# Quantised rows of the later chunk pairs: transposed by DMA in place of TensorE and ScalarE

## What is computed

```python
x = x + tanh(g_xattn[0]) * xattn(layernorm(x), ctx_1024, ctx_1024, Wq, bq, Wk, bk, Wv, bv, Wo, bo)
x = x + tanh(g_ffn[0]) * ffn(layernorm(x), w1, b1, w2, b2)

def _quant_per_tensor(x):
    scale = jnp.maximum(jnp.max(jnp.abs(x)), MIN_RANGE) / QP          # QP = 127
    return (_ste_round(x / scale), scale)
def _qlinear(x2d, w, b):
    xq, sx = _quant_per_tensor(x2d)
    wq, sw = _quant_per_tensor(w)
    out = jnp.matmul(xq, wq.T) + b[None, :]
    return out * (sw * sx)
h = gelu(_qlinear(x, w1, b1))          # 4096 x 2048
o = _qlinear(h, w2, b2)                # 4096 x 512
```

## Time and profile before

| | |
|---|---|
| three runs, us | 675.15, 672.69, 674.81; median 674.81 |
| profiled execution, us | 677.12, its span 675.2 |
| mean granted clock of TensorE | 0.955 |
| busy share of the span | PE 86%, DVE 74%, ACT 47%, POOL 27% |
| busy in step 0, 421.0 to 453.0 us | PE 31.01, DVE 23.11, ACT 24.84; DMA share 0.61 |
| in step 1, 453.0 to 482.9 | PE 29.84, DVE 27.67, ACT 23.07; DMA share 0.75 |
| in step 2, 482.9 to 513.7 | PE 30.70, DVE 29.72, ACT 23.07; DMA share 0.72 |
| in step 3, 513.7 to 541.5 | PE 27.80, DVE 21.91, ACT 19.26, POOL 11.12; DMA share 0.76 |

### The profile page before, as it was taken

One profiled execution on the slowest core, in us unless ns is written; L12 is line 12 of the kernel. 1 busy time (PEld: TensorE's weight loads), 2 busy tenths in 40 slices (PEclk: granted clock), 3 DMA queues, 4 the chain that ended last, 5 costly groups with the idle time before them and its releaser, 6 DMA issues. The chain is left out here.

```text
span 675.2 us, 9643 instructions
## 1 busy us (share of the span) xinstructions
PE 582.0 (86%) x3280; PEld 328.2 (49%) x3280; DVE 502.5 (74%) x718; ACT 318.4 (47%) x377; POOL 184.5 (27%) x160
## 2 busy tenths in 40 slices
PE   2889777999998899999999833999999909999998
PEld 2644535656646567565574521444444403444443
DVE  6568864988879888798677864689999719794262
ACT  1327157162362523625326134877777619565440
POOL 1007145160251421514204210000000530742272
PEclk9898978999999999999999975999999967999999
DMA  9903000520010010100101135577776767698763
GB/s 307 372 12 115 0 1 15 200 83 17 0 62 0 1 64 1 64 0 0 63 0 63 63 132 196 192 282 288 278 279 261 298 240 269 245 411 314 255 231 142
DMA packets 37088, 98.14 MB, mean 145 GB/s; under 512 B 2624, under 2 KB 3392, under 8 KB 32448
## 3 DMA queue, kind: packets, MB, share of 16 engines
q1 hardware_dynamic: 37056, 97.72, 38.9%
HBM read 55.77 MB, written 41.94 MB: 145 GB/s over the span
## 5 line engine op out<-in xcount | busy, mean ns | idle before, releaser
L1059 PE MATMUL ps<-h_sb,w_q 128*128 128x512 bf16 (+1 forms) x512 | 116.7, 383 | 2.4 <-ACT h_sb L1082 1.3
L1304 PE MATMUL ps<-w_q,h_q 128*128 128x512 bf16 x448 | 96.9, 379 | 0.0
L1059 PEld LDWEIGHTS ps<-h_sb,w_q 128*128 128x128 bf16 x512 | 49.3, 99 | 58.9 <-issue 4.9
L526 ACT ACTIVATE prob<-ps 77x1024 f32<-77x1024 f32 x64 | 62.6, 1018 | 24.5 <-PE ps L359 24.5
L1304 PEld LDWEIGHTS ps<-w_q,h_q 128*128 128x128 bf16 x448 | 43.8, 98 | 52.9
L900 POOL TENSOR_TENSOR c_lo<-c_sb,c_hi 128x512 fp32r<-128x512 f32 x32 | 45.1, 1424 | 84.9 <-ACT c_hi L539 84.9
L562 ACT ACTIVATE q_hi<-ps,bq_sb 128x512 fp32r<-128x512 f32 x32 | 22.0, 688 | 97.1 <-PE ps L320 97.1
L1097 ACT ACTIVATE xo<-ps,b1s,sc 128x1024 f32<-128x1024 f32 x48 | 57.8, 1205 | 18.6 <-PE ps L1059 17.5
L1167 DVE TENSOR_REDUCE hmax<-xo 128x1024 f32 (+1 forms) x48 | 57.2, 1213 | 11.6 <-ACT xo L1097 11.6
L909 POOL TENSOR_TENSOR x<-x,bo_gate 128x512 f32<-128x512 f32 (+1 forms) x32 | 45.1, 1417 | 73.7 <-DVE xn L658 70.0
L1382 POOL TENSOR_TENSOR xo<-xo,b2s 128x512 f32<-128x512 f32 x32 | 47.3, 1507 | 60.5 <-DMA xo<-x_dram 41.7
(11 more groups left out here) (126 smaller groups left out, 1047.8 us busy)
## 6 DMA issues: line engine op xcount, KB each, us to landing
h_dram<-xo SPq DMA_DIRECT2D x48, 512.0 KB, 2.7
h_sb<-h_dram SPq DMA_DIRECT2D x16, 1024.0 KB, 10.3
x<-in_x SPq DMA_DIRECT2D x8, 1024.0 KB, 5.3
x_dram<-x SPq DMA_DIRECT2D x8, 1024.0 KB, 3.9
xo<-x_dram SPq DMA_DIRECT2D x8, 1024.0 KB, 4.8
x<-h_dram SPq DMA_DIRECT2D x8, 1024.0 KB, 7.5
out<-xo SPq DMA_DIRECT2D x7, 1024.0 KB, 4.4
x<-in_w_t SPq DMA_DIRECT2D x1, 4096.0 KB, 19.9
```

The source lines that it names most:

```text
L526: nc.scalar.activation(prob[0:NK, p % SLOTS, :].rearrange("p (s n) -> p s n", s=2), ps[0:NK, 2 * (p % 2):2 * (p % 2) + 2, :], ACT.Exp).the ...
L1059: mm = nc.tensor.matmul(ps[:, 2 * (m % 2) + s, :], w1_q[:, k, m * P:(m + 1) * P], xq_t[:, one(2 * j + s), k, :], start=(k == 0), stop=(k = ...
L1304: mm = nc.tensor.matmul(ps[:, 4 * s + t, :], h_q[:, s, m, t * P:(t + 1) * P], w2_q[:, m, :], start=(m == 0), stop=(m == MF - 1))
```

## The change

The rows of the pairs of chunks 1, 2 and 3 (those that are prepared in steps 0 to 2) are no longer transposed by TensorE and copied by ScalarE. SP issues one transposing transfer for each row, from its slot of xq straight to its place in xq_t, 128 KB; as built, the instruction names blocks of 16 source rows by 128 columns. `T_AT` now tells SP's places: ahead of the store of tile 1, 3, 5, 7, 9, 11, 12 and 13, SP waits for that row's xq and issues the transfer. There is a semaphore for each of the four slots (`xqt_turned`); VectorE waits on it before it rounds a new row into the slot, and TensorE waits for all four at the start of steps 1 to 3. The first pair of chunks is transposed as before, and ScalarE's bank copies are left for it alone.

```diff
-    T_AT = (2, 4, 6, 8, 10, 12, 13, 14)
+    T_AT = (1, 3, 5, 7, 9, 11, 12, 13)
...
+        xqt_turned = [sem(f"xqt_turned{s}") for s in range(YS)]
...
                     for m in range(MF):
+                        if m in T_AT:
+                            u = T_AT.index(m)
+                            sp.wait_ge(xq_on, PT * (j + 1) + u + 1)
+                            apart(sp)
+                            sp.dma_start(xq_t[:, bass.ds(2 * (j + 1) + u // TT, 1), :, (u % TT) * P:(u % TT + 1) * P
+                                              ].rearrange("p o k n -> p (o k) n"), xq[:, u % YS, :],
+                                         transpose=True).then_inc(xqt_turned[u % YS], 16)
                         sp.wait_ge(h_on, MF * j + m + 1)
...
                 def step(j, first, last):
-                    pe.wait_ge(xqt_on, PT * j + PT)
+                    if first:
+                        pe.wait_ge(xqt_on, PT)
+                    else:
+                        for s in range(YS):
+                            pe.wait_ge(xqt_turned[s], 16 * (PT // YS) * j)
+                            apart(pe)
...
                         mm.then_inc(h_mm, 1)
-                        if m in T_AT and not last:
-                            transposes(PT * (j + 1) + T_AT.index(m), T_AT.index(m))
...
                             widen(MQ + PT + m)
-                        if m in T_AT and not last:
-                            transposed(j + 1, T_AT.index(m))
...
+                def turns(u, n):
+                    return (n - u) * (16 * (PT // YS) // PT) - 16 * (PT // YS) + (16 if u >= YS else 0)
...
                     dve.wait_ge(y_on, n + 1)
-                    if not isinstance(n, int) or n >= YS:
+                    if isinstance(n, int) and YS <= n < PT + YS:
                         dve.wait_ge(xqt_mm, n - YS + 1)
+                    elif isinstance(n, int) and n >= YS:
+                        dve.wait_ge(xqt_turned[u % YS], 16)
+                    elif not isinstance(n, int):
+                        dve.wait_ge(xqt_turned[u % YS], turns(u, n))
```

More of the change, by code:

```diff
@@ L1041, in transposes @@
                     pe.wait_ge(xq_on, n + 1)
-                    if not isinstance(n, int) or n >= 2:
+                    if n >= 2:
                         pe.wait_ge(xqt_on, n - 1)
```

## The result

The changed kernel took 683.6 us, the median of 4 runs (680.99 to 685.08), beside 673.94 for the kernel before in the same comparison: 9.7 us more by the medians. The ratio of the two is 1.013, 95% interval 1.010 to 1.016. The forecast was 674.1, no measurable change. The profiled execution of after has a span of 683.1 us, against 675.2.

A forecast was written before the change was run, and what follows sets the result against it. The hidden stage's end was taken to bound the run: w2m plus 29.0 gives 545.8, the last maximum plus 0.8 gives 546.3. The later, against 547.02, is -0.7 us, turning the median 674.81 into 674.1; range 672.3 to 688.

The forecast's parts named there:

- L: At each step start: time from the last xq to its transfer's landing, taken as 3.0 us, ends 1.7 and 4.7.
- (d): Starts of steps 1 to 3: TensorE waits for all eight transfers; step 1 1.2 us sooner, step 3 0.2.
- (c): SP's queue: 24 transfers at 0.5 us of engine time fit beside the stores; issues up to 1.5 us delay none.
- (e): TensorE before step 3: a 3.3 us hole halves the clock for eight matmuls, costing 1.7 us.
- (a): TensorE: 96 transposes gone save 1.7 us in step 0; the same in steps 1 and 2 is worth nothing.
- (b): ScalarE: 24 copies gone bring nothing, since it waits for TensorE or VectorE either way.
- rival 3: Whole stage: gain kept, landing near 2 us and clock not dropped, -1.5 to -2.1 us, 673.0; chance 0.12.
- Rival 1: DMA engines become the bound: decides from 1.01 us a transfer, +13 us at 1.55; slower, chance 0.24.
- rival 2: Step starts: transfers land late or SP is held; +4.4 us (679.2) at a landing time of 6; chance 0.12.
- (f): SP's stores behind its wait for xq: covered by some 3 us less VectorE's lag, so no cost.
- The cover of step 2's start: Start of step 2: VectorE has 7.3 us of work, first tile ready after 6.1, hiding landings up to 4.2 us.
- w2m plus 29.0: Stage's end: 29.0 us after the third pair's last w2m maximum, through GpSimd; forecast 516.8 + 29.0 = 545.8.

The follow-up runs named there:

- e3: Changed kernel plus 16 matmuls into an unused bank at the end of steps 0 to 2, keeping TensorE busy while it waits; 677.67 us.
- e10: Changed kernel with milder earlier tables for rows, transfers and w2m, the last transfer two tiles earlier; nothing left out; 672.34 us.
- e1: Changed kernel with no transposing by TensorE or DMA in steps 0 to 2, first pair's rows read throughout, outputs wrong; 674.3 us.
- e2: Changed kernel with all 24 transfers issued into unread chunks and TensorE waiting for none, outputs wrong; 673.08 us.
- e4: Changed kernel with tables moved earlier: rows at tiles 0 to 9, transfers at tiles 1 to 10, all 24 kept; 672.43 us.
- e9: Changed kernel with 12 transfers instead of 24, into unread chunks, TensorE waiting for none, outputs wrong; 671.63 us.
- e5: Kernel before, TensorE still transposing, with earlier tables for rows, transposes and w2m; 675.18 us.

## Why the prediction was wrong

The forecast was no change, 674.1 us; the measured time lies inside the range but on the side that had 0.36. Two steps of the working failed together: the landing L in (d), with SP's issue time in (c) behind it, and the clock in (e), which was charged once and with 1.7 us. The last maximum came 12.5 us later than before where 1.5 had been put down (0.2 sooner by the wait, 1.7 later by the clock); when the clock is kept (e3) 7.7 of the 12.5 are gone, and when the last transfer is issued two tiles earlier (e10) all of them.

- **(a) Transposes off TensorE, -1.7 us in step 0: right.** From step 0's start (419.19) to the end of its tile 15 (453.37 - 3.60 = 449.77) it is 30.6 us, against 32.15 to step 1's start before: -1.6. Some 0.3 of it is the clock, which stood at 0.50 for the first 2.6 us of step 0 in after and for 3.2 before.
- **(b) ScalarE's copies: nothing.** No run tests them by themselves. In steps 1 and 2 little can have come of their going (0.4 and 0.2 us in e1); of step 3's 3.3 us in e1 their share is open. That more than 2.1 us can't come out, as rival 3 has it, was wrong for a kernel whose steps wait for no row: it had left out how far TensorE and ScalarE run ahead of VectorE into step 3.
- **(c) X taken at 0.5, measured 1.0 us.** The nearest row (a store, with the same bytes at the same rate) misled: bytes alone don't set the price of this transfer. Rival 1's threshold was 1.01, and e2 has a DMA share of 1.02 just there, with 16 us of waits for stores. That it costs little at this point is as rival 1 had it. The Trainium skill (Advanced Engine Details and Errata, X-Bar Transpose (TRN2)) has these transfers as fast as regular ones; this case's trace does not agree, 1.0 us of the engines against 0.35 for a quarter of a store, which is as many bytes. The Trainium skill (VectorE: DVE Perf Modes, The three transpose paths) has 1309 ns for one 128x128 block. That can't simply be multiplied: four blocks landed 3.1 us after the issue and held the engines 1.0.
- **(d) is the step that failed first: L = 3.0.** Measured 6.5, 4.1 and 3.5. From the start of SP's issue to TensorE's first matmul it was 3.6, 3.7 and 3.2 us, so that part of the 3.0 was near. It left out the time from the row to the issue: 2.9 us at the end of step 0, where SP was still busy with the issues ahead of it, and 0.4 and 0.3 us at the ends of steps 1 and 2. Part (c) had let an issue of up to 1.5 us delay nothing, because SP has 1.7 us from tile to tile. The issue alone stayed under that (1.27 in the median, 2.2 at most), but with the store and the waits' instructions a tile takes SP 2.3. So rival 2's "SP is late" was true at the end of step 0. Part (f) asked what the stores lose by standing behind the transfers, and not what the last transfer loses by standing behind stores and other transfers.
- **The cover of step 2's start** was reckoned with a first tile of 1.73 us. At half clock it takes 8 x 0.426 = 3.4: 4.1 + 3.4 + 1.4 = 8.9 us, 1.6 over VectorE's 7.3. VectorE did stand 1.85 us there. Even the assumed L of 3.0 would have failed: 7.8.
- **(e) Clock: mechanism right, size and places off.** 12 to 14 matmuls at half pace and not 8, 2.7 us and not 1.7, and at three starts and not one. Part (e) itself said that holes stand before steps 2 and 3, and then charged only step 3. e3 puts the clock's share at 5.5 to 5.9 us of the run and at most 7.7 of the last maximum: this is the largest term that was mis-sized.
- **(f) Stores covered: they were not.** A store landed in a median of 3.3 us and at most 5.9, and ScalarE waited for stores 6.5 us in after and 20.2 in e10, where the working had some 3 us to spare. This is not the loss, since e10 with the longest of these waits has none of it.
- **The sum's "w2m plus 29.0"**: the pause in it depends on when SP's loads start. Had it been kept (553.9), the stage would still have ended with the last maximum. "Last maximum plus 0.8" measured 0.33 where the maximum is last.
- **Rival 2** was the right one in kind (the landing late), and too cheap because the clock was left out of it: at L of 3.5 to 6.5 the run lost 9.7 us, where it had +4.4 at 6. Its threshold of 5.4 doesn't come out of its own working either: 448.7 + L, two periods of 26.8 + L and 31.1 to the end make 533.4 + 3 L, which passes 547.02 from L = 4.5.

## What to carry to other kernels

When an engine's work is given to a queue, follow the last item of each batch: everything that stands ahead of it in the issuing engine's program, its issue time (the issues of a tile, added up, must fit into the tile's time), its landing, and then the first work behind the wait at the clock that the hole leaves. A batch hand-over with no slack turned lateness into a stop and a slow restart here, and the restart cost more than the stop; issuing the last item two tiles earlier got all of it back. Check too whether the engine relieved was the bound: with no transfers and no waits (e1) the last maximum came 5.7 us sooner, and with all 24 transfers well placed (e10) 0.2.

## What was not expected of the hardware

- A transposing transfer of 128 KB (bf16, 128x512, SBUF to SBUF) took 1.27 us of SP to issue, 1.0 us of all sixteen DMA engines, and landed 3.1 us after its issue; a plain store of 512 KB had 0.37, 1.39 and 2.7. In e2 (DMA share 1.02) the issue itself grew to a median of 1.81 us and a longest of 2.79; at a share of 1.00 in e4 and e10 its median was 1.39 and 1.35, so the share alone doesn't set it.
- After holes of 3.4 to 3.8 us TensorE was granted 0.50 (1.2 GHz of 2.4) for its next 12 to 14 matmuls; with matmuls in the hole (e3) it stayed at 1.00.
- GpSimd's pause between its all-reduce and its next instruction was 6.9 to 7.1 us when SP's loads of x and h came 2.3 us or more after the start of the all-reduce, 8.7 when they came 0.7 us after it (e9), and 11.0 to 12.9 when they came with it (before, e1, e5). From the last w2m, as in the table, that is 7.5 to 7.8, 9.3 and 11.7 to 13.5.
